# Transposing a head pair's attention output on TensorE instead of by DMA

## The reference, cut to what matters

```python
Qh = (queries @ Wq).reshape(n, t, HEADS, D_K)      # queries = layernorm(x)
Kh = (keys @ Wk).reshape(n, t, HEADS, D_K)         # keys = values = ctx
Vh = (values @ Wv).reshape(n, t, HEADS, D_V)
energy = jnp.einsum('nqhd,nkhd->nhqk', Qh, Kh) * scale
energy = jnp.where(mask == 0, -1e+20, energy)
attention = jax.nn.softmax(energy, axis=-1)
heads_out = jnp.einsum('nhqk,nkhd->nqhd', attention, Vh)
concat = heads_out.reshape(n, t, HEADS * D_V)
return concat @ Wo                                  # added to x
```

## Time and profile before

| | |
|---|---|
| median of 3 executions | 1197.81 us (1196.31 to 1199.81) |
| the profiled execution | 1199.81 us, span 1198.1 us |
| granted TensorE clock, mean of the span | 0.945 |
| busy share of the span | PE 90%, DVE 62%, ACT 56%, POOL 44% |
| attention phase 0 | start to about 523 us |

### The profile page before, as it was taken

The page is one execution under the profiler, slowest core; times in us unless marked ns, Lnnn a source line. Parts: engine busy times, 40 slices in busy tenths (PEclk is TensorE's granted clock), DMA queues, the critical chain, the costliest instruction groups (busy, mean ns, idle before and its releaser), DMA issues. The chain is left out here.

```text
span 1198.1 us, 28632 instructions
## 1 busy us (share of the span) xinstructions
PE 1072.4 (90%) x10229; PEld 789.5 (66%) x10230; DVE 748.1 (62%) x2152; ACT 675.9 (56%) x1282; POOL 526.3 (44%) x594
## 2 busy tenths in 40 slices
PE   5799999999999999976599999598988856999996
PEld 2566777777777777666388885344554444888885
DVE  5677887787778877956611115567777764555553
ACT  4787876687668877837232216366666632433331
POOL 4685455455544433210237640567666402223313
PEclk9899999999999999975799999899999966999998
DMA  9333333234333333243536535514445221112110
GB/s 309 104 77 69 82 87 80 63 78 93 73 80 72 86 69 70 67 151 120 187 132 186 176 62 195 177 55 135 133 116 152 81 88 31 28 28 34 23 18 10
DMA packets 120027, 116.16 MB, mean 97 GB/s; under 512 B 43488, under 2 KB 100064, under 8 KB 119776
## 3 DMA queue, kind: packets, MB, share of 16 engines
q1 hardware_dynamic: 112608, 105.27, 31.0%
q0 software_dynamic: 7296, 9.25, 4.5%
HBM read 59.89 MB, written 21.82 MB: 68 GB/s over the span
## 5 line engine op out<-in xcount | busy, mean ns | idle before, releaser
L556 ACT ACTIVATE e<-masked,neg_max 128x512 f32<-128x512 f32 x256 | 184.3, 720 | 44.7 <-DVE neg_max L655 43.6
L629 DVE TENSOR_TENSOR e_t_lo<-et,e_t_hi 128x512 f16<-128x512 f32 x256 | 176.6, 690 | 51.1 <-ACT e_t_hi L549 48.5
L655 DVE CUSTOM_DVE_ANT_0 masked<-sc,mask_bias 128x512 f32<-128x512 f32 x256 | 175.6, 686 | 40.3 <-issue 33.6
L549 ACT ACTIVATE e_t_hi<-et 128x512 f16<-128x512 f32 x256 | 151.3, 591 | 80.8 <-PE et L450 79.7
L450 PEld LDWEIGHTS et<-ident,e 128*128 128x128 f32 x1024 | 125.3, 141 | 56.8 <-issue 9.6
L450 PE MATMUL et<-ident,e 128*128 128x128 f32 x1024 | 154.8, 274 | 0.9 <-ACT e L556 0.8
L2085 ACT ACTIVATE d_e<-d_st 128x384 f32<-128x384 f32 (+1 forms) x192 | 93.8, 526 | 49.6 <-PE d_st L2226 45.0
L69 PE MATMUL ob<-v_lo,e_t_hi 128*128 128x65 f16 x1024 | 119.6, 193 | 0.0
L68 PE MATMUL ob<-v_hi,e_t_hi 128*128 128x65 f16 x1024 | 119.4, 193 | 0.0
L70 PE MATMUL ob<-v_hi,e_t_lo 128*128 128x65 f16 x1024 | 118.8, 193 | 0.0
L442 PE MATMUL sc<-kk,qq 128*128 128x512 f16 x256 | 97.2, 380 | 5.3 <-DVE neg_max L655 3.8
(11 more groups left out here) (442 smaller groups left out, 2744.7 us busy)
## 6 DMA issues: line engine op xcount, KB each, us to landing
kk<-nat_k SPq DMA_DIRECT2D x64, 256.0 KB, 3.5
raw<-in_fc SPq DMA_DIRECT2D x16, 1024.0 KB, 7.5
qq<-nat_q SPq DMA_DIRECT2D x64, 128.0 KB, 2.6
qk<-scratch_stack SPq DMA_DIRECT2D x64, 128.0 KB
mask_raw<-in_mask SPq DMA_DIRECT2D x16, 256.0 KB, 3.2
scratch_stack<-kq_hi SPq DMA_DIRECT2D x16, 256.0 KB, 3.1
scratch_stack<-kq_lo SPq DMA_DIRECT2D x16, 256.0 KB, 3.2
d_expert_raw<-in_gate_w SPq DMA_DIRECT2D x8, 512.0 KB, 3.7
```

The source lines that it names most:

```text
L549: nc.scalar.activation(e_t[u % NBUF].hi[:], et[u % 2][:], ACT.Copy).then_inc(turned_hi, 1)
L556: nc.scalar.activation(e[u % NBUF][:], masked[u % NBUF][:], ACT.Exp, bias=neg_max[:, g % 2, j:j + 1], scale=-1.0).then_inc(exp_ok, 1)
L629: nc.vector.tensor_tensor(e_t[u % NBUF].lo[:], et[u % 2][:], e_t[u % NBUF].hi[:], ALU.subtract).then_inc(turned_lo, 1)
L655: nc.vector.tensor_tensor_reduce(masked[u % NBUF][:], sc[j % 2][:], mask_bias[g // PAIRS % 2][:, j % QT, :], -SCALE0, 3e38, ALU.add, ALU.m ...
```

## The change

The outputs of pairs 0 to 30 become a new kind of side work `t`, done at j = 7 of the next pair (g = 1 to 31). PE transposes `o` in four f32 transposes into a `pj` bank (`turn_out`), ACT copies the bank to a `raw` buffer as it does for k, q and v, and POOL's `split` writes hi and lo straight into `o_t`. `split_out`, `turn_parts`, the buffers `o_hi` and `o_lo` and their semaphores go; `o` becomes two buffers, used in turn, so that DVE waits for the transposes of two pairs before, in place of the split of the last one. Consumers wait for the splits instead of the DMAs. At the end of the phase, the `pj` bank of the last turn is the one used for the third late output tile.

```diff
@@ side_work
+    if j == 7 and g >= 1:
+        return "t", g - 1
@@ buffers
-        o, o_parts = sb("o", [P, QT, P]), [sb(n, [P, QT, P], F16) for n in ("o_hi", "o_lo")]
+        o = [sb(f"o{i}", [P, QT, P]) for i in range(2)]
@@ sync
-                        sp.wait_ge(done, g + 1)
-                        sp.dma_start(whole[:, ct, :].rearrange("p (t n) -> p t n", n=P), part[:].rearrange("p t d -> p (t d)"), transpose=True).then_inc(out_turned, 16)
-                    if g >= 1:
-                        turn_parts(g - 1)
@@ gpsimd
+                    elif kind == "t":
+                        b, ct = at // PAIRS, at % PAIRS
...
+                        hi, lo = o_t[b % 2].hi[:, ct, :], o_t[b % 2].lo[:, ct, :]
-                def split_out(g):
-                    pool.wait_ge(normed, 2 * (g + 1))
-                    if g >= 1:
-                        pool.wait_ge(out_turned, TURNED * g)
-                    pool.tensor_copy(o_parts[0][:], o[:]).then_inc(out_hi, 1)
-                    pool.wait_ge(out_hi, g + 1)
-                    pool.tensor_tensor(o_parts[1][:], o[:], o_parts[0][:], ALU.subtract).then_inc(out_lo, 1)
-                        if j == 5 and g >= 1:
-                            split_out(g - 1)
@@ tensor
+                def turn_out(what):
+                    g = what[1]
+                    out = open_group(what)
+                    pe.wait_ge(normed, 2 * (g + 1))
+                    for qt in range(QT):
+                        mm = pe.transpose(out[:, qt * P:(qt + 1) * P], o[g % 2][:, qt, :], T.ident[:])
+                    mm.then_inc(pj_full, 1)
@@ project_out
-                    pe.wait_ge(out_turned, TURNED * (b + 1) * PAIRS)
+                    pe.wait_ge(split_done, COPY0["t", (b + 1) * PAIRS - 1] + 1)
@@ vector
-                    if a == 0 and g >= 1:
-                        dve.wait_ge(out_lo, g)
+                    if a == 0 and g >= 2:
+                        dve.wait_ge(pj_full, GROUP0["t", g - 2] + 1)
```

More of the change, by code:

```diff
@@ L156, in phase_attention0 @@
         mask_in, bias_ok = [sem(f"mask_in{i}") for i in range(2)], sem("bias_ok")
-        out_hi, out_lo, out_turned = sem("out_hi"), sem("out_lo"), sem("out_turned")
-        TURNED = 2 * 16
         last_turned, last_hi, last_lo, late_full = (sem(n) for n in ("last_turned", "last_hi", "last_lo", "late_full"))
-        late = [sc[0], sc[1], pj[0], ob[0][:].rearrange("p t d -> p (t d)")]
-        last_bank, last_part = pj[1], o_t[(B - 1) % 2]
+        before_last = GROUP0["t", PAIRS0 - 2] % 2
+        late = [sc[0], sc[1], pj[before_last], ob[0][:].rearrange("p t d -> p (t d)")]
+        last_bank, last_part = pj[1 - before_last], o_t[(B - 1) % 2]
         rstd, shift = sb("n_rstd", [P, NT]), sb("n_shift", [P, NT])
@@ L291, in _ @@
                         load_mask((g // PAIRS + 1) * QT + g % PAIRS)
-                    if g >= 1:
-                        turn_parts(g - 1)
-                turn_parts(PAIRS0 - 2)
             @block.gpsimd
@@ L316, in split @@
                         src = src.rearrange("p (h d) -> p h d", d=DK)
+                    elif kind == "t":
+                        b, ct = at // PAIRS, at % PAIRS
+                        if b >= 2:
+                            pool.wait_ge(pj_full, GROUP0["w", (b - 2, QT - 1)] + 1)
+                        if b < 2:
+                            pool.wait_ge(part_lo, PART0["wq_b" if at == 0 else "wq_c" if at == 1 else "wo_b"] + 1 - len(EARLY))
+                        hi, lo = o_t[b % 2].hi[:, ct, :], o_t[b % 2].lo[:, ct, :]
                     else:
@@ L428, in do_side_work @@
                         project_v(what)
+                    elif what[0] == "t":
+                        turn_out(what)
                     elif what[0] == "z":
@@ L502, in open_late @@
                     elif qt == 2:
-                        pe.wait_ge(copied, len(COPY0))
-                        pe.wait_ge(added, len(ADD0))
+                        pe.wait_ge(copied, COPY0["t", PAIRS0 - 2] + 1)
                     else:
                         pe.wait_ge(normed, 2 * PAIRS0 - 1)
-                    pe.wait_ge(out_turned, TURNED * (PAIRS0 - 2))
+                    pe.wait_ge(split_done, COPY0["t", PAIRS0 - 3] + 1)
                     late_products(qt, range(CT - 2))
@@ L526, in _ @@
                 for qt in range(QT):
-                    mm = pe.transpose(last_bank[:, qt * P:(qt + 1) * P], o[:, qt, :], T.ident[:])
+                    mm = pe.transpose(last_bank[:, qt * P:(qt + 1) * P], o[(PAIRS0 - 1) % 2][:, qt, :], T.ident[:])
                 mm.then_inc(last_turned, 1)
-                pe.wait_ge(out_turned, TURNED * (PAIRS0 - 1))
+                pe.wait_ge(split_done, COPY0["t", PAIRS0 - 2] + 1)
                 for qt in range(QT):
@@ L639, in normalize @@
                     dve.wait_ge(rden_ok, 2 * g + a + 1)
-                    nc.vector.tensor_tensor(o[:, :, a * DK:(a + 1) * DK], ob[a][:, :, 0:DK],
+                    nc.vector.tensor_tensor(o[g % 2][:, :, a * DK:(a + 1) * DK], ob[a][:, :, 0:DK],
                                             rden[a][:].unsqueeze(2).to_broadcast([P, QT, DK]), ALU.mult).then_inc(normed, 1)
```

## The result

The kernel after takes 1208.02 us at the median of five executions (1204.86 to 1210.69), before 1196.31. These two medians lie 11.7 us apart. It is 1.0086, 95% interval 1.0064 to 1.0108, so after is 10.3 us slower (7.7 to 12.9). I had forecast 1203.0 within 1198.5 to 1209.0, and slower by over 0.3% with a chance of 0.70. The sign is right and the time lies in the range, near its upper end; the size is off by a factor of almost two. The profiled execution of after takes 1208.57 us, its span is 1206.8.

A forecast was written before the change was run, and what follows sets the result against it. PE's instruction issue was taken to bound the attention phase's steady stretches. The terms +14.1 - 2.6 - 5.8 - 0.5 = +5.2 us took the median from 1197.8 to 1203.0 us, with an 8 in 10 range of 1198.5 to 1209.

The forecast's parts named there:

- The transposes on PE: Unit 7 of each pair: 30 groups of four f32 transposes lengthen PE's stream by 0.47 us each, +14.1 us.
- Absorbed: Pairs 24, 29, 30 and unit 0 after six pairs: PE's existing waits hide part of the groups, -2.6 us.
- DVE's wait: normalize's wait for POOL's o_lo goes: -5.8 us in the opening, pairs 2 to 4, and -0.5 at pair 17.
- rival 1: Opening: its stall stays or becomes pair 5's wait for stacked q; +8.2 to +11 us, chance 0.13.
- POOL and the ring: POOL's splits move from j = 5 to j = 7, sharing three raw buffers; cost 0.
- ACT's copy: 31 more copies of 0.584 us after the exponential of the next pair's unit 0, hidden; cost 0.
- rival 2: Unit 1: the q projection waits for ACT's copy of the bank in every pair; +12 us more, 1215, chance 0.07.
- Rival 3: Unit 7: more is hidden, a group costs 0.3 us instead of 0.47; +2.7 us, 1200.5, chance 0.17.
- rival 4: Unit 7: PE has room for the groups, only returned waits are seen; -6.3 us, 1191.5, chance 0.06.
- The forecast's own range: Whole kernel: the forecast without rivals, 1200.5 to 1205 us.
- the signs that I was to be wrong: Unit 7 not longer, PE waiting for qq at pair 5, q projections waiting for raw, or a gap bringing clock 0.50.
- The clock of 1.00: Per-unit transposes 0.11 us apart at clock 1.00: taken as not bearing out that transposes don't count as clock work.

The follow-up runs named there:

- The two fixes: Kernel after with the second v projection at unit 3 in pairs 1 to 3 and ACT's copy ahead of its unit's exponential: 1201.35 us, ratio 1.0059.

## Why the prediction was right, and where it was too low

- *The transposes on PE, +14.1.* Right: unit 7 is 1.70 us long, and one, four and eight transposes give 0.14, 0.47 and 0.90 us.
- *Absorbed, -2.6.* Right: the six openings fell from 2.73 to 2.53 (-1.2), and pairs 24, 29 and 30 take the whole group without getting longer (-1.4).
- *DVE's wait, -5.8, and -0.5 at pair 17.* Right in what was returned: the stalls and the half clock are gone, and pair 17 gave 0.4. I credited it to two `o` buffers, which is wrong; one buffer does the same. That nothing else would be late next held for POOL, so rival 1's wait for stacked q didn't come in after. It did not hold for the bank.
- *POOL and the ring, "Cost 0", and the banks, which had no term.* POOL and the ring held PE up nowhere, but the sum lacks a term for the banks: this step failed. I followed the bank that the new group uses on to the q projection, but did not count how the group shifts all banks behind it. Before, the k projection of unit 0 waited for the bank of the v projection at unit 4 of the pair before. With one more group between, it waits for that of the v projection at unit 6, behind the three pairs that have one and a group `t`, and there DVE is still reading. 3 x 0.62 = +1.9 us; moving that projection to unit 3 took off 1.9.
- *ACT's copy, "0.2 us of room in the worst place, elsewhere about 1".* The mechanism is that of rival 2, only smaller. I took the worst place from one row, pair 25, and did not look behind the z pairs. There DVE has z's low part to make first, so ACT's exponential and the copy behind it come late: 6 x 0.28 = +1.7. The trace of before had it already, in units (6,0) and (6,1). The exponential of unit (6,0) ends at 127.28 + 0.72 = 128.00, and a copy behind it would end at 128.58. The q projection starts at 127.80, with the group 0.47 later, at 128.27. So the rows foretold a wait of 0.3:

```profile
127.28 0.72 ACT L556 ACTIVATE e<-masked,neg_max 128x512 f32<-128x512 f32 x1
...
127.80 0.38 PE L68 MATMUL pj<-z_t_hi,wq_hi 128*128 128x512 f16 x1
```

  The same copy in pair 31, which has no projections to hide it, made unit 3 2.18 us long instead of 1.69: +0.5.

The whole by these terms: 14.1 - 2.6 - 5.8 - 0.4 + 1.9 + 1.7 + 0.5 = +9.4, against 9.3 measured on the phase. The two fixes take off 3.8 and leave 5.5. The rest of the measured 10.3 is within its interval. Rival 3 (more hidden) needed groups at 0.3 us, rival 4 (faster) under 0.09; they cost 0.47.

That the time fell into the range is partly luck. The forecast's own range ended at 1205, and only rival 1 stretched it to 1209. Its mechanism, the wait for stacked q, did not come in after; bank waits that no term or rival had in full filled the same space. Of the signs that I was to be wrong, one came in six pairs: q projections wait for `raw`, that is for ACT's copy. Pair 31 starts 9.5 us later than before, not 5, of which 0.5 is the later start of pair 1.

One reading of the prediction goes too far. The clock of 1.00 doesn't tell whether transposes count for it: in each unit matmuls stand between them, and no run here has transposes alone.

How much of the opening's 5.8 us was the half clock can be estimated from rows, though no run changes the clock alone. Unit (4,4), which follows the gap, lasts 4.23 us before and 2.53 after, and (4,5) 1.39 and 1.24. Of these 1.9 us, 0.2 were lost while the clock was still 1.00. That leaves about 1.7 for the clock.

## What to carry to other kernels

A transfer that nobody waited for was free here, and moving its work to the engine that sets the pace cost its full issue time in 27 of 30 places, however short the instructions are; only where that engine waited anyway was it hidden. When a step is inserted into a rotation of buffers, list for every later user which buffer it now waits for and who empties it last, in each kind of round and not only in the steady one. A wait found next to a change may be removable alone: here its order cost one line and gave 0.4%, while the change that removed it as well cost 0.9%.

## What the runs showed that I had not expected

- Extra PE work partly pays for itself by shortening waits that end at a fixed time: 0.43 us more per group in 30 groups made the phase 9.5 us longer instead of 13.0.
- From pair 1 on, the phase of after repeated within 0.01 us between two executions, while the part behind it varied by up to 7 us between kernels that don't differ there.
